# Second products of the shared passes as 512 + 256 columns over all four accumulator banks, four chunks behind, and seven idle matmuls at the start

## The reference, cut to what matters

```python
x = hidden_states
s0 = _dense(x, swi[0], swo[0])          # relu(x @ swi) @ swo, F = 1024
s1 = _dense(x, swi[1], swo[1])
h = jax.nn.relu(jnp.einsum('bsd,bdf->bsf', x, wi[type_label]))
eo = jnp.einsum('bsf,bfd->bsd', h, wo[type_label])
gate_in = jnp.concatenate([eo[:, 0], s0[:, 0], s1[:, 0]], axis=-1)
w = jax.nn.softmax(jax.nn.relu(gate_in @ g1) @ g2, axis=-1)[:, :, None, None]
return eo * w[:, 0] + s0 * w[:, 1] + s1 * w[:, 2]
...
x = x + _L0_cond_ref(x, ...)
x = x + _L1_cond_ref(x, zX, zY, zR, 1, 1)   # lap_x, lap_y and zR * y * (1 - y)
```

## Time and profile before

| | us |
|---|---|
| median of 3 runs | 1099.43 (1097.92 to 1099.93) |
| the profiled execution | 1099.38 |
| its span | 1097.8 |
| PE busy in the span | 1092.0 |
| DVE busy | 794.5 |
| ACT busy | 592.0 |

### The profile page before, as it was taken

The page is one execution under the profiler, slowest core; times in us unless marked ns, Lnnn a source line. Parts: engine busy times, 40 slices in busy tenths (PEclk is TensorE's granted clock), DMA queues, the critical chain, the costliest instruction groups (busy, mean ns, idle before and its releaser), DMA issues.

```text
span 1097.8 us, 21813 instructions
## 1 busy us (share of the span) xinstructions
PE 1092.0 (99%) x7864; PEld 1030.5 (94%) x7864; DVE 794.5 (72%) x1426; ACT 592.0 (54%) x1253; POOL 88.7 (8%) x130
## 2 busy tenths in 40 slices
PE   9999999999999999999999999999999999999998
PEld 7888888888888889999999999999999999999998
DVE  4666666666676634878777787788787787877876
ACT  2655566565565523555555555555555555555552
POOL 1211211221121004000000000000000000000001
PEclk9999999999999999999999999999999999999999
DMA  8666667666676425022021121120220220211100
GB/s 253 201 170 182 182 203 199 191 191 176 184 214 171 114 49 184 31 77 88 12 78 51 48 78 43 53 82 12 77 88 12 78 70 29 77 49 49 59 30 25
DMA packets 75613, 114.24 MB, mean 104 GB/s; under 512 B 9881, under 2 KB 53746, under 8 KB 75506
## 3 DMA queue, kind: packets, MB, share of 16 engines
q1 hardware_dynamic: 60402, 61.73, 19.1%
q0 software_dynamic: 13952, 50.60, 14.8%
q10 hardware_dynamic: 1152, 0.53, 0.2%
HBM read 91.49 MB, written 17.04 MB: 99 GB/s over the span
## 4 chain that ended last, share of the span: by engine, by line
PE 98%; DMA 1%; issue 0%; SPq 0%; DVE 0%; POOL 0%; POOLq 0%
PE acc L1364 11%; PE acc L1365 11%; PE acc L1363 11%; PE acc L1349 11%; PE hbank L1270 6%; PE hbank L1271 6%; PE hbank L1198 6%; PE hbank L1199 6%; PE hbank L1272 6%; PE hbank L1200 6%; PE acc L1350 5%; PE tbank L1271 3%; PE tbank L1270 3%; PE tbank L1272 2%; PE acc L1326 1%; PE acc L1251 1%
## 5 line engine op out<-in xcount | busy, mean ns | idle before, releaser
L1364 PE MATMUL acc<-swo,hh 128*128 128x256 f32 x992 | 280.0, 282 | 0.0
L1365 PE MATMUL acc<-swo,hl 128*128 128x256 f32 x992 | 279.8, 282 | 0.0
L1363 PE MATMUL acc<-swo,hh 128*128 128x256 f32 x992 | 279.3, 282 | 0.0
L852 DVE SCALAR_TENSOR_TENSOR hl<-hbank,hh 128x512 fp32r<-128x512 f32 (+1 forms) x184 | 111.0, 608 | 134.2 <-ACT hh L1471 134.1
L1471 ACT ACTIVATE hh<-hbank 128x512 fp32r<-128x512 f32 (+1 forms) x184 | 97.8, 534 | 182.2 <-PE hbank L1200 181.0
L1365 PEld LDWEIGHTS acc<-swo,hl 128*128 128x128 f32 x992 | 189.0, 191 | 0.0
L1364 PEld LDWEIGHTS acc<-swo,hh 128*128 128x128 f32 x992 | 188.5, 190 | 0.6
L1363 PEld LDWEIGHTS acc<-swo,hh 128*128 128x128 f32 x992 | 188.1, 190 | 0.6
L1349 PE MATMUL acc<-ewo,hh 128*128 128x512 f32 x496 | 180.1, 395 | 0.0
L1350 PE MATMUL acc<-ewo,hl 128*128 128x256 f32 x496 | 139.0, 280 | 0.0
L1349 PEld LDWEIGHTS acc<-ewo,hh 128*128 128x128 f32 x496 | 93.1, 188 | 21.2 <-DVE hl L852 0.2
(11 more groups left out here) (315 smaller groups left out, 2667.2 us busy)
## 6 DMA issues: line engine op xcount, KB each, us to landing
rw<-in_L_cond_wi POOLq DMA_DIRECT2D x44, 512.0 KB, 4.8
rw<-in_L_cond_wo POOLq DMA_DIRECT2D x44, 512.0 KB, 4.8
rw<-in_x_columns SPq DMA_DIRECT2D x16, 512.0 KB, 4.7
xs<-in_x SPq DMA_DIRECT2D x16, 512.0 KB, 4.1
ei<-eo_scratch SPq DMA_DIRECT2D x16, 512.0 KB, 4.9
xs<-in_x_columns SPq DMA_DIRECT2D x126, 64.0 KB, 3.3
out<-ot SPq DMA_DIRECT2D x15, 512.0 KB, 3.1
eo_scratch<-eo SPq DMA_DIRECT2D x100, 64.0 KB, 2.0
```

The costliest lines, as they stand in the source:

```text
L852: e.scalar_tensor_tensor(h_slot(HL, g), bank[:, 0:w], 0.0, h_slot(HH, g).bitcast(F32), ALU.max, ALU.subtract).then_inc(h_lo, 1)
L1363: e.matmul(to, hi, woc[:, f, 0:D], start=(c == 0 and j % 2 == 0), stop=False, skip_group_check=True)
L1364: e.matmul(to, hi, woc[:, f, D:2 * D], start=False, stop=False, skip_group_check=True)
L1365: return e.matmul(to, lo, woc[:, f, 0:D], start=False, stop=(c == NC - 1 and j % 2 == 1), skip_group_check=True)
```

## The change

Four things change. (1) In passes 26 to 54 (`spread_out`) a block's second product is one matmul of 512 columns (high by high and high by low side by side) and one of 256 (low by high, onto the second half). Each block has its own bank, so a pass now uses all four. (2) `add_shared` reads two banks at once and needs two instructions for each u: the first halves of both banks, then the second halves, the second waiting for the first. (3) The second products of these passes run `LONG_LAG` = 4 chunks behind, and the passes' other DVE work is placed anew: `add_shared` of the pass before goes to `c` = 3 (u = 0 ahead of the step's sums, u = 1 behind two of them), `column_sums` to `c` = 2, and `lap_x` to `lap_y` and ACT's `quadratic` one chunk later, `result` into chunk 0 of the next pass. Passes 55 and 56 number their banks anew. (4) `FILL` = (0, 7) adds seven matmuls of ones by ones behind the table products, and `swi[0]`'s first piece comes as one transfer.

```diff
-FILL = (0, 0)
+FILL = (0, 7)
...
+LONG_LAG = 4
+def behind(g):
+    old = g - LONG_LAG
+    return old if old >= AT_CHUNK[SEVENS[0], 0] - LAG else None
...
+def spread_out(n):
+    return paired(n) and n >= FIRST + 2
+def result_banks(n, u):
+    if spread_out(n):
+        return {2 * u, 2 * u + 1}
+    if paired(n):
+        return {2 * (n - FIRST) + u}
+    if n in HALVES:
+        return {{0: 0, 2: 1, 1: 2, 3: 3}[u]}
+    return {u}
...
-    return max([v for (m, w), v in ACC.items() if m < n and result_bank(m, w) == result_bank(n, u)], default=0)
+    return max([v for (m, w), v in ACC.items() if m < n and result_banks(m, w) & result_banks(n, u)], default=0)
...
+                if c == 3:
+                    add_shared(n - 1, 0)
                 top_right_sum(g)
                 low_right_sum(g)
+                if c == 3:
+                    add_shared(n - 1, 1)
                 top_low(g - 1)
...
+                high, low = (acc_all[:, 2 * u:2 * u + 2, i * D:(i + 1) * D] for i in range(2))
+                e.scalar_tensor_tensor(y, high, WB[:, 1 + b, t:t + 1], y, ALU.mult, ALU.add).then_inc(*V.up())
+                e.wait_ge(dve_seq, V.n)
+                e.scalar_tensor_tensor(y, low, WB[:, 1 + b, t:t + 1], y, ALU.mult, ALU.add).then_inc(acc_free, 1)
...
-                        if c == 2:
-                            add_shared(n - 1)
...
+                    if b == 1 and t >= 1 and c == 0:
+                        result(t - 1)
...
-                        if c == (5 if t < NT - 1 else 3):
-                            add_shared(n - 1)
+                        if not seven(n) and c == (5 if t < NT - 1 else 1):
+                            add_shared(n - 1, 0)
+                            add_shared(n - 1, 1)
...
-                        if c == (3 if t else 4):
+                        if c == (2 if t else 4):
                             column_sums(t + 1)
...
-                if c == 1:
-                    second_product(g - LAG, (0, 1))
+                if c == 3:
+                    second_product(behind(g), (0, 1))
...
+                if spread_out(n):
+                    e.matmul(acc[j][:, 0:2 * D], hi, woc[:, f, :], start=(c == 0), stop=False)
+                    return e.matmul(acc[j][:, D:2 * D], lo, woc[:, f, 0:D], start=False, stop=(c == NC - 1))
...
+                if (n, c) == (SEVENS[-1] + 1, 0):
+                    for old in range(g - LONG_LAG, g - LAG):
+                        second_product(old)
...
-                    if (i, p) == (0, 0):
-                        for c in range(4):
-                            cs = slice(c * 128, (c + 1) * 128)
-                            e.dma_start(raw_rows(0, 0)[:, :, cs], src[:, :, cs]).then_inc(w_chunk[c], 16)
-                        continue
```

More of the change, by code:

```diff
@@ L366, in cond_resid_program @@
         tbank = ctx.enter_context(nc.psum_tensor("tbank", [128, 512], F32))
-        acc = [ctx.enter_context(nc.psum_tensor(f"acc{i}", [128, 512], F32)) for i in range(4)]
+        acc_all = ctx.enter_context(nc.psum_tensor("acc", [128, 4, 512], F32))
+        acc = [acc_all[:, i, :] for i in range(4)]
         h_prod = sem("h_prod")
@@ L384, in cond_resid_program @@
         w_in = [[sem(f"w_in{i}{p}") for p in range(4)] for i in range(2)]
-        w_chunk = [sem(f"w_chunk{c}") for c in range(4)]
         u_in = [[sem(f"u_in{i}{p}") for p in range(4)] for i in range(2)]
@@ L865, in evacuate, with add_shared @@
                     e.tensor_tensor(dst, acc[j][:, D:2 * D], dst, ALU.add).then_inc(acc_free, 1)
-            def add_shared(n):
+            def add_shared(n, u):
                 t, b = PASSES[n][1] // 2, PASSES[n][1] % 2
[L870 to L877, removed]
-                                           WB[:, 1 + b, t:t + 1], y, ALU.mult, ALU.add).then_inc(acc_free, 1)
+                y = inner(t)[:, 2 * u:2 * u + 2, :]
+                e.wait_ge(acc_done, ACC[n, u])
+                if b == 0:
+                    e.wait_ge(dve_seq, AT["residual", t])
+                else:
+                    e.wait_ge(acc_free, ACC[n - 1, u])
+                if not spread_out(n):
+                    e.scalar_tensor_tensor(y, acc[result_bank(n, u)].rearrange("p (j d) -> p j d", j=2),
+                                           WB[:, 1 + b, t:t + 1], y, ALU.mult, ALU.add).then_inc(acc_free, 1)
+                    return
+                high, low = (acc_all[:, 2 * u:2 * u + 2, i * D:(i + 1) * D] for i in range(2))
+                e.scalar_tensor_tensor(y, high, WB[:, 1 + b, t:t + 1], y, ALU.mult, ALU.add).then_inc(*V.up())
+                e.wait_ge(dve_seq, V.n)
+                e.scalar_tensor_tensor(y, low, WB[:, 1 + b, t:t + 1], y, ALU.mult, ALU.add).then_inc(acc_free, 1)
             def cut_low(ws, p):
@@ L1073, in _ @@
                     if b == 0 and t >= 1:
-                        if c == 2:
-                            add_shared(n - 1)
-                        if c == 3:
+                        if c == 4:
                             lap_x(t - 1)
-                        if c == 4:
+                        if c == 5:
                             react(t - 1)
-                        if c == 5:
+                        if c == 6:
                             add_x(t - 1)
-                        if c == 6:
+                        if c == 7:
                             lap_y(t - 1)
-                        if c == 7:
-                            result(t - 1)
+                    if b == 1 and t >= 1 and c == 0:
+                        result(t - 1)
                     if b == 1:
@@ L1296, in seven_step @@
                     of_sum(other, 3, y[0][1], True, False).then_inc(h_prod, 1)
-                    second_product(g - LAG, (0, 1))
+                    if behind(g) is not None:
+                        second_product(behind(g), (0, 1))
                     e.wait_ge(p_copy, 4 * q + 1)
                     of_sum(corner, 0, y[0][0], False, False).then_inc(p_prod, 1)
-                    second_product(g - LAG, (2, 3))
+                    if behind(g) is not None:
+                        second_product(behind(g), (2, 3))
                     return
-                if c == 1:
-                    second_product(g - LAG, (0, 1))
+                if c == 3:
+                    second_product(behind(g), (0, 1))
                 e.wait_ge(p_copy, 4 * q + 2)
@@ L1307, in seven_step @@
                 of_sum(corner, 2, y[1][1], False, False).then_inc(p_prod, 1)
-                second_product(g - LAG, (2, 3) if c == 1 else None)
+                if behind(g) is not None:
+                    second_product(behind(g), (2, 3) if c == 3 else None)
                 e.wait_ge(p_copy, 4 * q + 4)
@@ L1622, in _ @@
                     last_quadratic(2 * (c - 4))
-                if FIRST < n < NP and PASSES[n][1] % 2 == 0 and c == 3:
+                if FIRST < n < NP and PASSES[n][1] % 2 == 0 and c == 4:
                     quadratic(PASSES[n][1] // 2 - 1)
```

12 lines of the change are left out of this document (3 added, 9 removed).

## The result

The changed kernel takes 1113.69 us (median of 4 runs, 1112.68 to 1114.87), beside 1099.68 for the kernel before on the same chip: 1.0136 times as long, 95% interval 1.0124 to 1.0148. The forecast was 1111.0, 11.4 more than before; by the ratio the change cost 15.0. The profiled execution took 1114.04 us, its span is 1112.5, 14.7 more than the span before.

The account below looks back on a forecast made before the run. PE, busy without a gap in the seven-product passes, was taken to bound the kernel, with DVE at 80%. Terms -7.0 + 16.4 + 0.8 + 0.5 + 1.7 - 1.0 = +11.4 gave 1111 us, range 1098 to 1118.

Parts of the forecast that it names:

- DVE's chain in b = 1 passes: Chunks 2 to 4: late additions and `top_right_sum` stall PE 0.84 and 0.33 us, 1.17 in each of 14 passes, +16.4 us.
- P: PE's start of chunk 2 in a pass, from which the forecast counts DVE's and PE's times.
- b = 0 passes: 15 passes without 1024-column work in chunks 2 and 3: a tie before block 2, 0.05 each, +0.8 us (0 to 2).
- Joined matmuls: Second products on PE, 928 blocks: 512 + 256 columns save 0.0075 us a block, -7.0 us (-5.9 to -8.8).
- Pass 26: First two steps: no second products before ACT's copies, exposing up to 0.35 + 0.7 us once, +0.5 us.
- Handoff to pass 55: Pass 55 needs pass 54's banks at once and waits for DVE's additions: +1.7 us (0.8 to 2).
- The start: Idle matmuls and single transfer before chunk 4: PE's higher rate comes sooner, -1.0 us (-1.5 to +1.6).
- the break: PE's stand from about 8.15 to 9.50 us for `swo`, which the idle matmuls close so the rate rises sooner.
- Rival 4: At the start the idle matmuls only delay, the rate rising no earlier: +2.6 us, 1113.6 us; chance 20%.
- Rival 1: DVE keeps up in b = 1 passes, both stalls go and the kernel is faster: 1092 us; chance 10%.

Follow-up runs that it names:

- e2: The changed kernel with one addition for each u, the second halves of the accumulator banks left out of the result: 1094.21 us, ratio 0.9957 to the kernel before.
- e4: The changed kernel with DVE's other work in b = 1 passes moved to later steps and the last `residual` one pass ahead: 1098.06 us, ratio 0.9996.
- e6: The changed kernel with `top_right_sum` ahead of the first pair of additions instead of behind it: 1121.09 us, ratio 1.0196 to the kernel before.
- e8: e4 with DVE's additions in step 3 interleaved with the two sums, so dependent additions are separated: 1093.88 us, ratio 0.9960 to the kernel before.
- e9: e8 with each block's second product as three matmuls of 256 columns again: 1101.27 us, ratio 1.0025 to the kernel before.
- e1: The kernel before with the new start alone (seven idle matmuls, single transfer): 1097.38 us beside 1098.48, ratio 0.9990.
- e7: The changed kernel without the seven idle matmuls, the single transfer kept: 1112.49 us, ratio 1.0135 to the kernel before.
- e11: e8 without the seven idle matmuls: 1094.08 us, ratio 0.9958 to the kernel before.
- e5: The changed kernel run again unaltered, as yardstick for e6 to e8: 1113.06 us, ratio 1.0132 to the kernel before.
- e10: The kernel before with `swi[0]`'s first piece as one transfer, no idle matmuls: 1098.42 us beside 1098.45, ratio 0.9998.
- e3: The changed kernel with three matmuls of 256 columns for each block again, into the same banks: 1116.03 us, ratio 1.0165 to the kernel before.

## Why the prediction was right, step by step

The sign, the place and the size were right: 1113.7 against a forecast of 1111.0, range 1098 to 1118.

**DVE's chain in b = 1 passes** held to a few hundredths. With P = 642.65: `column_sums` at P + 4.07 (forecast 4.10), the additions at 4.87 and 5.65 (4.89, 5.66), `top_right_sum` at 6.32 (6.32), the last addition ended at P + 8.51 (8.49). PE continued at P + 6.79 (6.85) and at 8.57 (8.6). The loss of such a pass is 1.22 instead of 1.17. I had put 0.1 between the end of DVE's work and PE's start; it is 0.06, and the 0.10 stand behind the late matmul instead. Behind the product into `other` they vanish in the wait for block 2, whose date DVE sets; behind block 2 they are lost, and I had nothing there. In pass 27, the first, it is 0.7. Together +16.6 against +16.4. e2 shows that the doubled additions are needed for it, e4 that the other work in chunks 2 and 3 is, and e6 that the order of the sum and the first pair alone does not help.

**b = 0 passes**: 0.08 in each of 14 (pass 26 is counted by itself), +1.1 (+0.8). In pass 34 the last addition ended at P + 7.37 and PE started block 2 at P + 7.46 (forecast 7.3 and 7.43).

**Joined matmuls**: -6.4 by e8 and e9, within the bounds, the chosen -7.0 slightly too large.

**Pass 26**: 0.89 and twice 0.10, +1.1 (+0.5). The sum of two exposed copies was mis-sized: the 0.35 and 0.7 named were 0.26 and 0.63, and I took half of them.

**Handoff to pass 55**: +2.0 (+1.7, up to 2). The rows:

```profile
1081.25 1.27 DVE L917 SCALAR_TENSOR_TENSOR y<-ei,wb,xs 128x1024 f32<-128x1024 f32 x1
1082.64 0.75 DVE L903 SCALAR_TENSOR_TENSOR y<-acc,wb,y 128x512 f32<-128x512 f32 x1
1083.43 0.75 DVE L905 SCALAR_TENSOR_TENSOR y<-acc,wb,y 128x512 f32<-128x512 f32 x1
...
1084.32 0.36 PE L1403 MATMUL acc<-swo,hh 128*128 128x256 f32 x1 [1.74 <-DVE y L905]
```

**The start**: -1.9 in the profile (first matmul with `ewh` at 23.61 instead of 25.48), -1.1 by e1's median (-1.0). The size was right, the mechanism was not shown, and that the two agree is partly luck: in the four profiles with seven idle matmuls and the late rise this matmul starts at 24.94 to 25.75, which is no gain to speak of. I let the break be the only thing that keeps the rate low; e7 and e11 reach about the same times as e5 and e8 without idle matmuls, and e10 shows what the break can do when it is 2 us long. Rival 4's price of +2.6 appears in no profile, but its mechanism, idle matmuls that only delay, is not refuted: at an equal rise of the rate they do (0.5 to 1.7 us at chunk 4). Which part of the new start gains the 1.1 is open: the single transfer alone (e10) and taking away the idle matmuls (e7, e11) each gave nothing that can be told from none, and idle matmuls alone were not run.

**Not foreseen**: the end. From the last matmul of the stretch above to the last instruction it takes 38.0 us instead of 31.2. Of these 6.8, 2.8 are the eight blocks moved out behind it (a shift and no cost), 2.0 the handoff, and 2.1 lie behind PE's last second product and come with the wait for border rows. e5 has 1.2 there. In the first profile the last border transfer is issued 2.0 us late, and DVE goes on 1.7 us after its issue. In e3 to e9 and e11, all with both additions, it is issued in time, but DVE goes on only 2.6 to 2.9 us after it, a wait of 0.6 to 0.9. In the kernel before, e1 and e2 DVE does not wait. In e10, the kernel before but for one transfer at the start, it waits 0.70, as the issue of the first two border transfers took 2.19 us instead of 1.45; so a wait here does not need the second additions. What makes these transfers late stays open.

**The sum** as measured: -6.4 + 16.6 + 1.1 + 1.1 + 2.0 - 1.9 + 2.1 = +14.6, against 14.7 in the spans. For e5, with -2.1 at the start and 1.2 at the end, the same sum gives 13.5 against 13.7. The sum is 3.2 above the forecast's 11.4: 2.1 of it the end, 0.6 pass 26, 0.6 joining, 0.3 the handoff, 0.5 the passes, less 0.9 for the start. The two largest of these, the end and the start, differ from profile to profile and happen to cancel in part. Rival 1 (DVE keeps up) is what e8 makes of it: 1093.9, where that rival's sum was 1092.

## What to carry to other kernels

Before a shared engine with spare time on average gets more work, lay its list beside the bounding engine's at the fullest place and add up start-to-start distances: 80% busy hid a stall of 1.2 us in every second pass, and the sum found it to 0.05. When the work fits on average but not there, move what nobody waits for (e4, -15 us) and put something independent between two dependent operations (e8, 3 us less in these passes), rather than only change the order of the critical few (e6, 6 us more in them). A gain on the bounding engine is measured best in a kernel in which it never waits: the same edit cost 3 us in e3 and 7 in e9.

## What the runs showed of the hardware

- A matmul whose weight load waited for a semaphore delays the next one by another 0.10 us (649.44 to 649.66, 0.22 instead of 0.12), and by 0.08 when the semaphore came only just in time (e4, 669.00 to 669.30, 0.30 instead of 0.23).
- Two dependent additions of 128x512 on DVE stand 0.78 apart (647.52 to 648.30), an independent operation follows after 0.67 (648.30 to 648.97). Reading 256 columns of each of two banks costs the same as 512 of one: 745 and 751 ns (means of L903 and L905 in the seven-product passes) against 743 in the earlier trace rows.
- The rate of PE rose at 4.8 to 5.5 us in some profiles and at 9.7 to 10.9 us in others (13.1 in the kernel before), though PE's work was the same up to about 5 us. For an equal number of idle matmuls chunk 4 moved by 1.5 to 2.7 us with it. A stand of 2.03 us soon after an early rise was followed by a fall to the lower level (e10), one of 0.91 us was not (e7).
